# A first chunk kept apart, the next chunk's convolution ahead of the transposes, weights in two loads, and idle products at the start

## The reference

```
conv = conv_b + causal depthwise convolution of x with 128 taps, cond, one filter per channel
proj = conv @ Wp + bp                     # 512 -> 2*64
B, C = softplus(proj[..., :64]), tanh(proj[..., 64:])
u    = x @ Ws + bs                        # 512 -> 64
s_t  = decay * s_{t-1} + dt * B_t * u_t   # scan over time
x    = x + (C * s) @ Wo + bo
h_t  = tanh(h_{t-1} @ Wh + x_t @ Wx + b)  # scan over time, h_0 = cond
x    = x + h
```

## Time and profile before

| what | time |
|---|---|
| median of 3 runs | 1177.9 us (1176.81 to 1179.24) |
| profiled execution | 1177.63 us |
| its span, first to last instruction | 1175.8 us |
| PE busy | 1157.7 us, 98% of the span |
| PEld, DVE, ACT, POOL busy | 969.3, 697.0, 569.6, 350.8 us |
| the chain that ended last | PE 96%, DVE 2%, DMA 1% of the span |

### The profile page before, as it was taken

How to read it: one execution, slowest core, us unless ns; L and a number is a source line. 1 busy time by engine, 2 the same in 40 slices (tenths; PEclk the granted TensorE clock), 3 DMA queues, 4 the chain that set the end, 5 groups by cost and what they waited for, 6 DMA issues and landing times.

```text
span 1175.8 us, 16134 instructions
## 1 busy us (share of the span) xinstructions
PE 1157.7 (98%) x5984; PEld 969.3 (82%) x5984; DVE 697.0 (59%) x1110; ACT 569.6 (48%) x836; POOL 350.8 (30%) x200
## 2 busy tenths in 40 slices
PE   7899999999999999999999999999999999999997
PEld 7899999975788888888888888888888888888886
DVE  6566767667555555565565665555556556555553
ACT  3555665575354454535454545445354445454431
POOL 4300005022133333333333333333333333333330
PEclk9999999999999999999999999999999999999999
DMA  9888777712022232222222222222222222222202
GB/s 298 251 285 288 253 256 246 249 37 81 1 72 72 74 99 87 89 80 71 71 71 71 71 71 71 71 71 90 91 86 90 71 71 71 71 71 72 72 36 72
DMA packets 73746, 130.12 MB, mean 111 GB/s; under 512 B 3888, under 2 KB 32048, under 8 KB 73712
## 3 DMA queue, kind: packets, MB, share of 16 engines
q1 hardware_dynamic: 73712, 129.65, 34.7%
HBM read 96.08 MB, written 33.55 MB: 110 GB/s over the span
## 4 chain that ended last, share of the span: by engine, by line
PE 96%; DVE 2%; DMA 1%; POOL 0%; issue 0%; ACT 0%; POOLq 0%; SPq 0%; DVEq 0%
PE bank L836 10%; PE bank L844 10%; PE bank L845 10%; PE bank L830 10%; PE bank L848 10%; PE bank L829 10%; PE bank L755 10%; PE bank L770 5%; PE bank L884 5%; PE bank L805 3%; PE bank L811 3%; PE bank L819 2%; PE bank L820 2%; PE bank L784 2%; PE bank L786 2%; PE bank L783 2%
## 5 line engine op out<-in xcount | busy, mean ns | idle before, releaser
L399 POOL TENSOR_TENSOR x_lo<-x_f,x_hi 128x512 fp32r<-128x512 f32 x128 | 161.7, 1293 | 588.0 <-ACT x_hi L490 588.0
L517 ACT ACTIVATE h_f<-z_f 128x512 f32<-128x512 f32 x128 | 80.9, 632 | 296.5 <-DVE z_f L702 296.5
L844 PE MATMUL bank<-wh_hi,hT_hi 128*128 128x512 f32 x512 | 200.6, 392 | 0.0
L845 PE MATMUL bank<-wh_lo,hT_hi 128*128 128x512 f32 x512 | 200.0, 391 | 0.0
L830 PE MATMUL bank<-wx_lo,x_hi 128*128 128x512 f32 x512 | 199.7, 390 | 0.0
L829 PE MATMUL bank<-wx_hi,x_hi 128*128 128x512 f32 x512 | 199.6, 390 | 0.0
L711 DVE TENSOR_TENSOR hT_lo<-bank,hT_hi 128x512 fp32r<-128x512 f32 x128 | 88.5, 692 | 186.8 <-ACT hT_hi L521 186.8
L702 DVE TENSOR_TENSOR z_f<-bank,b_rows 128x512 f32<-128x512 f32 x128 | 88.5, 692 | 131.9 <-PE bank L848 128.6
L393 POOL TENSOR_TENSOR x_lo<-x_f,x_hi 128x2048 fp32r<-128x2048 f32 x32 | 147.7, 4615 | 1.4 <-PE bank L755 1.3
L755 PE MATMUL bank<-ring 128*128 128x128 f32 x1024 | 137.6, 280 | 8.1 <-DMA ring<-x_rev 7.3
L836 PE MATMUL bank<-wx_hi,x_lo 128*128 128x512 f32 x512 | 144.7, 404 | 0.3 <-POOL x_lo L399 0.3
(11 more groups left out here) (83 smaller groups left out, 1637.6 us busy)
## 6 DMA issues: line engine op xcount, KB each, us to landing
ring<-x_rev SPq DMA_DIRECT2D x64, 512.0 KB, 5.2
x_f<-x_dtb SPq DMA_DIRECT2D x32, 1024.0 KB, 8.2
out<-x_f SPq DMA_DIRECT2D x31, 1024.0 KB, 5.5
ring<-hankel SPq DMA_DIRECT2D x44, 512.0 KB, 4.1
ring<-hankel SPq DMA_DIRECT2D x20, 128.0 KB, 4.6
wx_f<-Wx SPq DMA_DIRECT2D x1, 1024.0 KB, 8.2
wh_f<-Wh SPq DMA_DIRECT2D x1, 1024.0 KB, 8.0
out<-x_f SPq DMA_DIRECT2D x4, 256.0 KB, 2.2
```

Source lines behind the costliest of these rows:

```text
L399: nc.gpsimd.tensor_tensor(x1_lo[:, c], x1_f[par][:, c], f(x1_hi[:, c]), ALU.subtract)\
L517: nc.scalar.activation(h_f[:], z_f[:], ACT.Tanh).then_inc(h_ready, 1)
L844: nc.tensor.matmul(z, hT_hi[:, k], wh_hi[:, k], start=False, stop=False)
L845: nc.tensor.matmul(z, hT_hi[:, k], wh_lo[:, k], start=False, stop=False)
```

## The change

Chunk 0 is copied into the room of `bc`, channel last, which `add_proj(0, m)` overwrites bank by bank behind `turn(0, m)`. So `conv` is free when block 0 ends, and block 1's order on PE becomes convolution, transposes, products. ACT copies the convolution bank ahead of the turned one there, and the shift of ring step 17 moves on ACT and DVE from the last banks of block 0 into block 1. Chunk 2 keeps its layout. Wp's first chunk is loaded where all of Wp was, the other three behind ring step 18; POOL splits them in two parts, and PE waits for each part at its first use. Eight products of the identity with itself, into a bank that nobody reads, stand at the head of PE's list.

```diff
+WARM = 8
         def conv_room(c, m):
-            if c % 2 == 0:
+            if c == 0:
+                return bc[:].rearrange("p (t d) -> p t d", t=TIME)[:, :, bass.ts(m, PER_BANK)]
+            if c == 2:
                 return conv[:, bass.ts(m, PER_BANK)]
             return conv[:, :, bass.ts(m, PER_BANK)]
...
         def conv_at(c, t):
-            return conv[:, :, t] if c % 2 == 0 else conv[:, t]
+            if c == 0:
+                return bc[:, bass.ts(t, P)]
+            return conv[:, :, t] if c == 2 else conv[:, t]
...
-            sp.dma_start(wp_f[:], Wp.rearrange("(c p) n -> p c n", p=P)).then_inc(wp_loaded, DMA)
+            wp_rows = Wp.rearrange("(c p) n -> p c n", p=P)
+            sp.dma_start(wp_f[:, 0:1], wp_rows[:, 0:1]).then_inc(wp_loaded, DMA)
             for n in range(RING, D // CH):
                 sp.wait_ge(conv_done, CH // PER_BANK * (n - RING + 1))
                 load_ring(n, n % RING)
+                if n == 18:
+                    sp.dma_start(wp_f[:, 1:KC], wp_rows[:, 1:KC]).then_inc(wp_loaded, DMA)
...
         # ACT
             for m in range(0, BANKS, 2):
-                shift(m // 2 + 2)
+                if m < BANKS - 2:
+                    shift(m // 2 + 2)
                 copy_conv(0, m)
-            for c in range(KC - 1):
+            for m in range(BANKS):
+                copy_conv(1, m)
+                copy_turned(0, m)
+                if m % 2 == 0 and m // 2 + BANKS // 2 + 1 < SHIFTED:
+                    shift(m // 2 + BANKS // 2 + 1)
+            for c in range(1, KC - 1):
                 for m in range(BANKS):
                     copy_turned(c, m)
-                    if c == 0 and m % 2 == 0 and m // 2 + BANKS // 2 + 2 < SHIFTED:
-                        shift(m // 2 + BANKS // 2 + 2)
                     copy_conv(c + 1, m)
...
         # PE
+            for _ in range(WARM):
+                nc.tensor.matmul(TURN[0][:, 0:P], ident[:], ident[:], start=True, stop=True)
             for m in range(BANKS):
                 convolution(0, m)
-            pe.wait_ge(wp_loaded, DMA)
-            pe.wait_ge(wp_ready, 2)
-            for c in range(KC - 1):
+            for m in range(BANKS):
+                convolution(1, m)
+                turn(0, m)
+                if m > 0:
+                    project(0, m - 1)
+            project(0, BANKS - 1)
+            for c in range(1, KC - 1):
```

More of the change, by code:

```diff
@@ L343, in shift @@
                 if n > 10:
-                    pool.wait_ge(wp_ready, 2 if n > 13 else 1)
+                    pool.wait_ge(wp_ready, 2)
                 pool.wait_ge(t_loaded[slot], DMA * (n // RING + 1))
@@ L352, in _ @@
                     pool.wait_ge(shifted_pool, n + 1)
-                    nc.gpsimd.tensor_copy(wp_hi[:], wp_f[:, 0:LAST]).then_inc(wp_ready, 1)
-                if n == 13:
+                    nc.gpsimd.tensor_copy(wp_hi[:, 0], wp_f[:, 0]).then_inc(wp_ready, 1)
                     pool.wait_ge(wp_ready, 1)
-                    pool.wait_ge(shifted_pool, n + 1)
-                    nc.gpsimd.tensor_tensor(wp_lo[:], wp_f[:, 0:LAST], f(wp_hi[:]), ALU.subtract).then_inc(wp_ready, 1)
+                    nc.gpsimd.tensor_tensor(wp_lo[:, 0], wp_f[:, 0], f(wp_hi[:, 0]), ALU.subtract).then_inc(wp_ready, 1)
             pool.wait_ge(shifted_pool, SHIFTED)
+            pool.wait_ge(wp_loaded, 2 * DMA)
+            nc.gpsimd.tensor_copy(wp_hi[:, 1:LAST], wp_f[:, 1:LAST]).then_inc(wp_ready, 1)
+            pool.wait_ge(wp_ready, 3)
+            nc.gpsimd.tensor_tensor(wp_lo[:, 1:LAST], wp_f[:, 1:LAST], f(wp_hi[:, 1:LAST]), ALU.subtract).then_inc(wp_ready, 1)
             pool.wait_ge(ws_wo_loaded, 2 * DMA)
@@ L595, in _ @@
             for m in range(1, BANKS, 2):
-                shift(m // 2 + 2)
+                if m < BANKS - 1:
+                    shift(m // 2 + 2)
                 copy_conv(0, m)
@@ L600, in _ @@
                     turn_rest_of(c, m)
-                    if c == 0 and m % 2 == 0 and m // 2 + BANKS // 2 + 2 < SHIFTED:
-                        shift(m // 2 + BANKS // 2 + 2)
+                    if c == 0 and m % 2 == 0 and m // 2 + BANKS // 2 + 1 < SHIFTED:
+                        shift(m // 2 + BANKS // 2 + 1)
                     if m > 0:
@@ L746, in convolution @@
                         pe.wait_ge(x_part_loaded[slot], DMA * (n // RING + 1))
+                    if d % PER_BANK == 0 and c == 1 and m < 4:
+                        if m % 2 == 0:
+                            pe.wait_ge(conv_copied_act, (BANKS - 4 + m) // 2 + 1)
+                        else:
+                            pe.wait_ge(conv_copied_dve, (BANKS - 4 + m) // 2 + 1)
                     if d % PER_BANK == 0 and m >= 4:
@@ L765, in turn @@
                     pe.wait_ge(turn_copied, BANKS * c + m - 2)
+                    if m == 0:
+                        pe.wait_ge(wp_loaded, 2 * DMA)
                     if m == 2:
@@ L781, in project @@
                 hi, lo = turned_hl[:, 0, n % 2], turned_hl[:, 1, n % 2]
+                if n == 0 and c < 2:
+                    pe.wait_ge(wp_ready, 2 * (c + 1))
                 pe.wait_ge(turn_copied, BANKS * c + n + 1)
```

## The result

The changed kernel takes 1171.88 us (median of 6 runs, 1170.72 to 1172.83) against 1177.94 (6 runs, 1176.8 to 1179.61) before: a ratio of 0.9948 [0.9935, 0.9960], or 6.1 us less. The forecast was 1170.3, in a range of 1167.8 to 1174.1. The profiled execution took 1172.83 us, the longest of its six; its span is 1171.0, 4.8 us shorter than before.

A forecast was written before the change was run, and what follows sets the result against it. TensorE was taken to bound blocks 2 and 3, with full transfer engines limiting block 0 and a hole behind it. Terms summed to -7.43 us from 1177.63, giving 1170.2, stated as 1170.3; range 1167.8 to 1174.1.

The forecast's parts named there:

- (3): Block 1: chunk 0 with channels side by side makes transpose weight loads as fast as block 2's, -3.93 us.
- Rival C: Block 1: slower products behind transposes, or bc loads colliding with writes, cancel the layout's gain; 1174.1 us, chance 0.11.
- (1): Behind block 0: TensorE starts with a convolution instead of waiting for the last copy, idle 2.08 to 0.25, -1.83 us.
- rival E: Behind block 0: ring step 16 lands later, so hole and low clock stay; 1173.6 us, chance 0.07.
- (2): Start of block 1: with the idle hole shortened, the slow clock behind it goes, -1.58 us.
- (4): Block 1: the new order's own waits, +0.63 us at its end and +0.20 at its start.
- (5): Block 0: three quarters of Wp leave the queue ahead of ring step 4, later loads land earlier, -0.92 us.
- no earlier than 41: Sign of a wrong prediction: block 0 ending no earlier than 41 us, where about 40.3 was expected.
- (6): Start of block 0: idle products lift the clock, but ring step 2 still waits for VectorE's shift, 0 us.
- (7): Block 0: copying chunk 0 in strided form costs ScalarE and VectorE no time, 0 us.
- Rival D: Block 0: VectorE's strided copies lengthen each ring step; 1181.4 us at 2.3 us a copy, chance 0.05.
- with the terms' bounds: Whole kernel: the forecast's own range from its terms' bounds, 1167.8 to 1172.5 us.

The follow-up runs named there:

- third series: Changed kernel (1172.88 us) beside three variants of it: no idle products (1173.33), old order with new layout (1172.78), late rates with order fixes (1169.89).
- second and third series: Here, the changed kernel rerun unmodified beside other variants: 1173.21 us, then 1172.88 us.
- the filled hole: Kernel before, with eight idle identity products put between block 0 and the first transposes: 1177.07 us, ratio 0.9984.
- first series: Here, the changed kernel without its eight idle products, run without the changed kernel itself beside it: 1174.2 us, ratio 0.9955.
- straight copies: Changed kernel with chunk 0's banks copied straight into bc, so turned wrongly and only timed: 1173.09 us, ratio 0.9957.
- late rates: Changed kernel with the decay rates' small ScalarE and VectorE instructions moved from the start to the middle of block 0: 1172.63 us, ratio 0.9948.

## Why the prediction came out right

- **(3), the layout, -3.93:** shown. Weight loads of 241 ns became 139, and 69.48 us became 65.55. It is the greater part of the gain, and in the third series the kernel with the layout and the old order has all of the changed kernel's gain. Rival C falls with it: a bank of block 1 takes 2.05 us (103.69 to 105.74), one of block 2 2.047.
- **(1), the hole, 2.08 to 0.25:** wrong in size. In the profile after it is 1.22, 0.97 more than forecast, and 0.8 of that is the later landing of step 16. The step that failed is the landing: it was taken from one execution, as if it were the kernel's. In the changed kernel's three profiles a ring step in the second half of block 0 takes 2.24 to 2.39 us, over all profiles 2.0 to 2.65, for nearly the same loads. In its profiles of the second and third series the first bank of block 1 follows block 0 with no hole to speak of (24 rows in one stretch from 39.80, third series); the longest wait for loads stands ahead of ring step 15 or 14 instead (1.30 and 0.89 us). This is rival E in part, without its low clock.
- **(2), the half clock, -1.58:** size confirmed in the kernel before, 1.53 by the filled hole. But the reason given for losing it, the order that closes the hole, is not shown: with the old order and the new layout the holes are 1.67 and 1.83 us and no half clock follows them either. That the term came was in part luck. The changed order has no half clock to save beside the layout, and its own waits take back what it saves of the hole, so it is worth nothing measurable (1172.78 against 1172.88); the forecast had 2.58 for (1), (2) and (4) together. Why the hole is shorter with the new layout, and why 2.08 us idle were followed by the half clock and 1.83 were not, is open.
- **(4), the order's own waits, +0.83:** three products in a row take 0.69 us (174.00 to 174.69, the end of block 2). Those of block 1's last bank could follow the product of 107.54 some 0.24 us later and be through at 108.47; they are at 109.19, 0.72 late where 0.63 was forecast. At the start two banks of 65.50 / 32 = 2.047 us, less the three products that the first has not, are 3.40; from 42.42 to 46.34 it took 3.92, 0.52 late and not 0.20. The shift of step 17 stands behind the first low part on VectorE (45.72 to 46.14), and the convolution waits for it. In all 66.77 us against 65.50: +1.27, and 1.9 in the profile of the third series.
- **(5), Wp in two loads, -0.92:** this is the term that was mis-sized: no run shows a gain, and block 0 ends at 41.20 and not at about 40.3, which the prediction itself had named as a sign of being wrong ("no earlier than 41"). Its own bound of 0 named the reason: the loads are late for their issue. The convolution of step 2 issues step 6, and the same shift of VectorE that makes term (6) nothing holds that convolution. I argued (6) from this gate and forgot it in (5).
- **(6), the idle products, 0:** borne out in the third series, to 0.45 us with overlapping ranges; the 1.3 us of the first series are left unexplained. The products took 3.78 us and not the 3.0 reckoned, yet block 0 started no later (5.22, before 5.37). The rows after them are faster (5.01 against 5.93 us for 32), and TensorE then waits for the shift that ends at 11.30. Step 6's x part, which waits for step 2's convolution, is issued at 14.26 without the idle products and at 14.12 with them (third series). The Trainium skill's "TensorE: Matmul & The Clock Gate" (What's actually happening) has the clock throttled by default and released by activity. The faster rows agree with it, but the granted clock doesn't show it: its column reads 1.00 there with and without the products.
- **(7), strided copies, 0:** shown, 692 ns against 692 and 586 against 589. Rival D falls. What "Advanced Engine Details and Errata", PSUM Cachelines, of the Trainium skill says of matmuls, that non-contiguous PSUM access slows them significantly, does not carry over to these copies.

Against the profiled span of before the change took 4.8 us off where 7.4 were foreseen: the misses are 0.97 at the hole, 0.44 in the waits of block 1, 0.92 for Wp less the 0.06 by which block 0 ended earlier, and 0.36 behind block 1, which no step spoke of. All four lie on the slow side. This profile was the kernel's longest run; the median lies 0.95 us below it, 1.6 us from the forecast instead of 2.5. The range came out right, but its upper end of 1172.5 "with the terms' bounds" does not follow from them: taken together the bounds of (1) to (5) reach at least from 1168.9 to beyond 1177.

Open is why the transfers take 2.24 to 2.39 us a step in one and the same kernel, and 2.0 to 2.65 in kernels with nearly the same loads. Over the eight steps from 8 to 16 that may be much of the spread of 1 to 2 us each way between runs, which is not shown; neither the straight copies nor the late rates settled it.

## What to carry to other kernels

Lay out what a transpose reads so that a weight load finds its numbers side by side, and price it from two stages of the same trace that differ in nothing else: that was the one term exact to the hundredth. Before booking a transfer that leaves a queue early, ask which engine's step issues the next ones: behind a gate in program order, here some small operations on VectorE ahead of a shift, the saved bytes only empty the queue. Moving these operations and removing the waits at a stage's two ends gained another 3 us together. And take a term out of the finished change again before calling it the cause: the new order, well argued from the trace before, brought nothing here beside the layout.

## What was unexpected of the hardware

A weight load of 128 x 128 fp32 takes 139, 205 and 241 ns with strides of 1, 4 and 128 numbers, where I had thought of two cases. The granted clock fell, from 2.4 to 1.2 GHz, behind idle stretches of 2.08 us (before, behind block 0: 0.62 on the mean of the next 4.44 us) and 2.02 us (old order with the new layout, ahead of step 2: 0.57 on the mean of 12 to 16 us). It did not behind 1.67 and 1.83 us, nor behind 1.98 and 2.01 us ahead of step 2 in the changed kernel of the second and third series, so the length of the idle stretch alone does not tell.
